# Mask products in pairs, new orders of the attention slots, and block ends without GpSimd's drain, in a one-core attention and routed-expert kernel on Trainium2

## The reference, cut to what matters

```python
def layer(x):                                  # (16, 512, 128)
    n = layernorm(x)
    q, k, v = split(einsum('bsd,ndh->bnsh', n, W_qkv))      # 16 heads of 8
    s = einsum('bnqh,bnkh->bnqk', q, k) / sqrt(8) + causal_mask * -1e10
    x = x + out_projection(softmax(s) @ v, W_out)
    z = layernorm(x)
    p = softmax(z @ Wr + br);  w, i = top_k(p, 2);  w = w / sum(w)
    return x + sum over the 2 chosen experts of w * expert_i(z)
```

## Time and profile before

| what | value |
|---|---|
| runs | 1258.79, 1259.54 and 1265.87 us, median 1259.54 |
| the profiled execution | 1261.42 us, its span 1259.7 us |
| span by stage | attention to about 790 us, tail and routing to 824, experts to 1212, sum to the end |
| PE busy from 50 to 650 us | 582.5 of 600 us, granted clock 1.00 (2.4 GHz) |
| DVE, ACT, POOL busy there | 467.5, 352.5 and 411.8 us |
| one batch (4 slots) in the steady state | 46.1 us for the batch from 484.92 to 531.04 us |

### The profile page before, as it was taken

How to read it: one execution, slowest core, us unless ns; L and a number is a source line. 1 busy time by engine, 2 the same in 40 slices (tenths; PEclk the granted TensorE clock), 3 DMA queues, 4 the chain that set the end, 5 groups by cost and what they waited for, 6 DMA issues and landing times. The chain is left out here.

```text
span 1259.7 us, 27452 instructions
## 1 busy us (share of the span) xinstructions
PE 1118.3 (89%) x8654; PEld 824.5 (65%) x8654; DVE 981.5 (78%) x2792; ACT 759.3 (60%) x1672; POOL 788.7 (63%) x1455
## 2 busy tenths in 40 slices
PE   3899999999999999999999998169999999999920
PEld 2565655655656566566556554169999999999910
DVE  4776877878778778778778873758888888888858
ACT  1465655555556556555555654268888888888800
POOL 2257485686686587677577677616666666666630
PEclk9999999999999999999999998579999999999965
DMA  5223545424424434433433421521111111111138
GB/s 146 92 74 111 175 129 162 133 87 126 137 87 134 124 95 123 130 100 116 135 99 107 130 57 42 153 66 52 52 52 53 52 52 52 52 52 52 31 120 301
DMA packets 138269, 127.37 MB, mean 101 GB/s; under 512 B 71848, under 2 KB 96432, under 8 KB 138128
## 3 DMA queue, kind: packets, MB, share of 16 engines
q1 hardware_dynamic: 127184, 103.59, 27.9%
q0 software_dynamic: 8640, 17.84, 4.4%
q10 hardware_dynamic: 2304, 4.20, 0.9%
HBM read 71.13 MB, written 54.43 MB: 100 GB/s over the span
## 5 line engine op out<-in xcount | busy, mean ns | idle before, releaser
L803 ACT ACTIVATE probs<-st 128x384 f32<-128x384 f32 (+1 forms) x768 | 396.7, 527 | 266.5 <-PE st L704 249.7
L844 DVE TENSOR_REDUCE neg_max<-sa 128x2 fp32r<-128x1024 f32 (+3 forms) x384 | 396.0, 1034 | 99.5 <-PE sa L689 97.5
L645 POOL TENSOR_SCALAR_AFFINE_SELECT probs<-probs 128x128 f32<-128x128 f32 (+1 forms) x768 | 244.2, 333 | 208.3 <-ACT probs L803 202.6
L704 PE MATMUL st<-q_stack,k_pad 128*128 128x256 f32 (+2 forms) x1024 | 355.4, 388 | 8.8 <-DMA q_stack<-max_scratch 6.7
L686 PE MATMUL sa<-k_pad,q_stack 128*128 128x256 f32 (+2 forms) x1024 | 334.7, 369 | 15.0 <-DVE neg_max L844 7.5
L686 PEld LDWEIGHTS sa<-k_pad,q_stack 128*128 128x128 f32 x1024 | 179.7, 191 | 118.1 <-issue 87.2
L704 PEld LDWEIGHTS st<-q_stack,k_pad 128*128 128x128 f32 x1024 | 182.2, 198 | 16.1 <-DMA q_stack<-max_scratch 7.9
L689 PE MATMUL sa<-maskneg,identb 128*128 128x128 bf16 (+1 forms) x768 | 191.6, 249 | 0.0
L1001 POOL DMA_INDIRECT y_scratch<-z,to_row x142 | 168.8, 1189 | 35.9 <-issue 35.9
L1035 PE MATMUL up<-xt_hi,w_cur 128*128 128x256 f32 x568 | 167.3, 295 | 0.0
L717 PE MATMUL pv<-probs,v_aug 128*32 128x512 f32 (+3 forms) x2048 | 167.3, 446 | 0.0
(11 more groups left out here) (159 smaller groups left out, 1536.7 us busy)
## 6 DMA issues: line engine op xcount, KB each, us to landing
q_stack<-q_scratch SPq DMA_DIRECT2D x64, 256.0 KB, 2.7
k_pad<-k_scratch SPq DMA_DIRECT2D x256, 64.0 KB, 2.4
xg<-rows_scratch SPq DMA_DIRECT2D x71, 130.0 KB, 2.1
q_scratch<-q_hi SPq DMA_DIRECT2D x16, 512.0 KB, 3.1
k_scratch<-k_hi SPq DMA_DIRECT2D x16, 512.0 KB, 3.0
y<-y_scratch SPq DMA_DIRECT2D x16, 512.0 KB, 5.4
q_scratch<-q_lo SPq DMA_DIRECT2D x17, 256.0 KB, 3.1
k_scratch<-k_lo SPq DMA_DIRECT2D x17, 256.0 KB, 3.3
```

What stands on the lines that cost most here:

```text
L645: pool.affine_select(out=blk, in_=blk, compare_op=ALU.is_ge, fill=0.0, base=0, pattern=[[0, w], [1, P]], channel_multiplier=-1).then_inc(m ...
L704: last = nc.tensor.matmul(st[:, t % 2, at:at + w], k_pad[:, G * g + j, kk * P:(kk + 1) * P], q_stack[:, g, S - w:S], start=True, stop=True)
L803: nc.scalar.activation(probs[:, n % 2, j, lo:lo + w], st[:, k % 2, at:at + w], ACT.Exp).then_inc(exp_done, 1)
L844: V.tensor_reduce(neg_max[:, n % 2, heads[0]:heads[-1] + 1, i], scores[:, :, 0:(i + 1) * P], AX.X, ALU.max, negate=True).then_inc(sa_read, 1)
```

## The change

Three edits. In `a_step` the first bank's mask product no longer follows the first bank's scores: both mask products come behind the second bank's scores, one after the other. In all four rows of `SLOT` tokens move. And the first two blocks are opened with `no_gpsimd_drain=True`: POOL's DRAIN is gone from their ends, and the four other engines' drains stand there as before.

```diff
-            1: "SR A0 B0 a0 B1 PV0 out S0 A1 B2 a1 B3 mT mE A2 S1 B4 mW a2 B5 A3 S2 B6 a3 B7 ln2 A4 B8 S3 PV1 PV2 PV3 OT a4 B9 mR rs2 A5 B10 RC a5 B11 ON zn",
+            1: "SR A0 B0 a0 Rf B1 PV0 A1 B2 out a1 B3 mT mE A2 S0 B4 mW a2 B5 A3 S1 B6 a3 B7 ln2 A4 B8 S2 PV1 PV2 PV3 a4 OT B9 mR rs2 A5 B10 RC a5 B11 ON zn",
...
-        block = route.enter_context(nc.Block())
+        block = route.enter_context(nc.Block(no_gpsimd_drain=True))
...
-                diagonal = sa[:, s % 2, bank, :].rearrange("p (e k) -> p e k", e=each)[:, :, i * P:(i + 1) * P]
-                last = nc.tensor.matmul(diagonal, identb[:, :], maskneg[:, :].unsqueeze(1).broadcast_to([P, each, P]),
-                                        start=False, stop=True, skip_group_check=True)
                 if bank == 1:
+                    for b2 in range(2):
+                        diagonal = sa[:, s % 2, b2, :].rearrange("p (e k) -> p e k", e=each)[:, :, i * P:(i + 1) * P]
+                        last = nc.tensor.matmul(diagonal, identb[:, :],
+                                                maskneg[:, :].unsqueeze(1).broadcast_to([P, each, P]),
+                                                start=False, stop=True, skip_group_check=True)
                     last.then_inc(sa_written, 1)
...
-        block = experts.enter_context(nc.Block())
+        block = experts.enter_context(nc.Block(no_gpsimd_drain=True))
```

## The result

The changed kernel takes 1244.69 us (median of 4 runs, 1243.33 to 1245.08) beside 1259.95 for the kernel before. The ratio is 0.9851, 95% interval 0.9831 to 0.9871. It is faster by 1.5%, inside the stated range, but the gain is smaller than the forecast 1235: the profiled execution went from 1261.42 to 1244.57, 16.9 us where the sum said 24.7.

The account below looks back on a forecast made before the run. PE was taken to set attention's pace, so gains had to be its idle or hidden lost time; 1.38 us a batch times 15.5 is 21.4, with 3.35 for drains 24.7 off 1261.4, as median 1235 us; range 1211 to 1252.

Parts of the forecast that it names:

- xT: Slot 3's transpose no longer waits for POOL's xn, worked one stage earlier; 0.55 us gained a batch.
- pairs: Attention steps: paired masks leave one exposed weight load instead of two; 0.24 us a slot, 0.54 a batch.
- POOL chain: Slot 1 into slot 2: POOL's work from out to zn sets zT at +15.62; PE's stretch 0.26 us longer.
- drains: Block ends without POOL's drain: 2.9 us gained after the expert block, 0.45 after the first.
- CM: Slot 0: CM behind a4 starts without its gap behind B7; 0.2 us gained a batch.
- PE products at the turn of a slot: Turns of slots 0, 2 and 3: next A0 no longer waits for OT; 0.6 us gained a batch.
- Rival 2: Attention steps: mask pairs save nothing, 8.4 us less gain, about 1243 us; chance 0.15.
- rival 1: Slot 1 to zT: POOL chain does not decide, another 1.24 us a batch gained, about 1216 us; chance 0.16.
- SP's chain: Into B0 of slot 1: later stores, earlier mR and earlier PE add 0.25 us of wait a batch.
- The forecast is wrong if zT does not wait (then it is too slow): PE timeline sign: zT should be the largest wait, near 1 us a batch; otherwise the forecast is too slow.
- Rival 3: Slot 1: AR and XL loads land too late and hold out; about 1276 us if 3.5 us later; chance 0.07.

Follow-up runs that it names:

- e4: Changed kernel with OT back ahead of a4 in all four slots; 1250.82 us, ratio 0.9915 to the kernel before.
- e5: Changed kernel with POOL's scattered stores S0 and S1 directly behind out in slot 1, S4 directly behind S3 in slot 2; 1245.12 us, ratio 0.9828.
- e3: Kernel before with the four new SLOT rows alone, masks and drains as before; 1254.54 us, ratio 0.9937.
- e8: Changed kernel with V behind PV0 in slot 0 and K ahead of a4 in slot 3; 1251.74 us, ratio 0.9902.
- e1: Kernel before with only the two POOL drains left out of the block ends; 1260.23 us, ratio 0.9978.
- e2: Kernel before with only the mask products in pairs, its own slots and drains kept; 1259.94 us, ratio 0.9971.
- b3: Kernel of e7 with store S2 moved from slot 1 to slot 2, S2 to S4 together there; 1239.63 us, ratio 0.9775.
- e7: Changed kernel with SR moved behind mW in slot 0; 1236.52 us, ratio 0.9778 to the kernel before.
- b1: Kernel of e7 with Rf behind mE in slot 1, S2 moved to slot 2, S2 to S4 together there; 1244.28 us, ratio 0.9824.
- b4: Changed kernel with SR behind mW in slot 0 and S4 directly behind S3 in slot 2; 1235.17 us, ratio 0.9766.
- e6: Changed kernel with a4 ahead of PV3 in slots 1 and 2, OT still behind both; 1245.73 us, ratio 0.9843.

## Why the prediction was right, and where its sum was wrong

- **Faster by over 1%:** right, and the range held the time. Of the mechanisms, xT, the pairs, the POOL chain and the drains came about; the turn of slot 2 and CM did not. The sum was 8 us too large. Against before's trace a batch gained 0.53 less than forecast: the turns of slots 0, 2 and 3 fell short by 0.43, CM by about 0.35, and K's copy cost 0.12, while the stretch to zT came out 0.41 better than its two terms.
- **PE products at the turn of a slot, 0.6 a batch:** the step that failed is "With a4 ahead of OT ... A0 of the next slot no longer waits for OT's time". A0 waits for step 4's maximum, 1.23 us of its own; OT in front only added to that. Measured against before, in the mean: slot 0 -0.18, slot 3 -0.12, slot 2 +0.13, so 0.17. In slots 0 and 3 it was CM and K behind a4 that covered the maximum, for with OT in front they still do (e4). In slot 2 A0 still stands 0.67 behind B11, 0.33 more than in slot 3, since a store of POOL ends just before the maximum (e5).
- **CM, 0.2:** its gap went (what follows B7 comes after 0.26 in place of 0.46), but from B7 to A5 slot 0 takes 3.66 us in place of 3.50, and 3.61 with the slots alone (e3). The gap had covered ACT's copy of V: B8 follows A4 after 0.52 in place of 0.36, and with V moved away it is 0.34 (e8). The step put no name to what that gap hid.
- **xT, 0.55:** it came in before's trace, where B5 to xT went from 0.81 to 0.28 in the mean. But in e1, with the same attention, it is 0.28 already, and the turn of slot 2 takes 1.14. The prediction added the two as if each had its own time. Together the turns and xT gained 0.70 against before's trace and 0.77 against e1's, where the forecast had 1.15.
- **Pairs, 0.24 a slot:** right in the sum, wrong in the parts. The first step of slot 1, in the changed kernel:

```profile
522.54 0.42 PE L687 MATMUL sa<-k_pad,q_stack 128*128 128x512 f32 x1
522.80 0.39 PE L707 MATMUL st<-q_stack,k_pad 128*128 128x512 f32 x1
523.02 0.40 PE L687 MATMUL sa<-k_pad,q_stack 128*128 128x512 f32 x1
523.26 0.28 PE L692 MATMUL sa<-maskneg,identb 128*128 128x128 bf16 x2
523.36 0.47 PE L707 MATMUL st<-q_stack,k_pad 128*128 128x512 f32 x1
523.76 0.64 PE L720 MATMUL pv<-probs,v_aug 128*32 128x512 f32 x4
```

  From A0 to PV0 it takes 1.22 us, before 1.36 (519.50 to 520.86). Two masks take 0.10, which is their 256 columns at 2.4 GHz alone, and a full product behind a full one 0.22 to 0.26 in place of 0.31. Over all batches without a wait step 0 gained 0.15 in slots 0 and 1 and 0.07 in slots 2 and 3 (0.08 with pairs alone, e2), steps 1 and 3 gained about 0.07 each, steps 2 and 5 nothing, and step 4 nothing or a loss of up to 0.08. Rival 2 is out: the steps got shorter, and loads for the full array are hidden here behind products of 512 columns, which alone are 0.21. The rule of the Trainium skill ("TensorE: Matmul & The Clock Gate", Part 3, "Packing small matmuls — row/col tiling") that a load overlaps only where row groups differ does not describe these rows.
- **The POOL chain, +0.26:** `out` starts at +3.92 and zT at +15.25 in batches where B0 does not wait (forecast 4.05 and 15.62); from `out` to the end of zn it is 11.2 us, worked out as 11.32. zT follows zn's end by 0.14 to 0.17 in 11 of 12 batches, so the chain does set it, and rival 1 fell. But its wait is short (B5 to zT 0.52 in place of 0.28 in the mean), because PE was held up on its way: A3 of slot 1 by Rf, which stands ahead of step 1's maximum now and had no term, and A0 of slot 2. In b3, where zT does not wait, it comes at +15.1, not at +14.4. The sign "The forecast is wrong if zT does not wait (then it is too slow)" failed: zT's wait came out small and the time was above 1235, not below. A3 in a batch where B0 did not wait (0.19 in the mean of all):

```profile
527.73 0.45 PE L687 MATMUL sa<-k_pad,q_stack 128*128 128x384 f32 x1 [0.46 <-DVE neg_max L847]
```

- **SP's chain, +0.25:** right in sign, by one trace each: B0's wait went from 3.9/11 = 0.35 to 4.9/11 = 0.45 booked. The step named the queue but not the cheap way out, SR behind mW (e7).
- **K behind a4:** no term. K's copy on ACT delays B9's exponential, and B11 waits for it: from A5 to B11 slot 3 takes 1.00 us in place of 0.87, 0.12 of its missing 0.3.
- **Drains, 3.35:** 2.8 by e1's ratio, with 2.9 and 0.2 in its trace and 2.3 and 0.4 in the changed kernel's.
- **Rival 3:** did not come about, and it waited for the wrong load. In the kernel's code XL of a batch loads the x that `out` adds one batch later; only AR's loads belong to the `out` that follows them. The trace agrees: in one batch `out` starts at +5.14 and the XL issued ahead of it lands at +5.34. AR's loads land at +4.25 at the latest, and `out` starts directly behind the zeroing ahead of it in 11 of 12 batches. It starts at up to +5.9 where B0 waits, but B0's wait had moved all of the slot by nearly as much (1.89 of the 1.99).

## What to carry to other kernels

When a wait names an instruction, read that instruction's own length before crediting the edit that clears the queue in front of it: here the 1.2 us of the maximum stayed. Two waits on one path may stand in for one another, so read them in a second trace of the same program before adding them. A gap that goes has to be followed to the next product on each other engine, since short waits hide one another, and an engine that is busy for only 59% of the time, as ACT is here, can be the next one. And in a queue worked in order, a wait for something slow (SR for its stores) belongs behind what is ready (mW).

## What the runs showed of the hardware that was not expected

- A DVE instruction that waited for PE and came due when a scattered store of POOL was ending or had just ended started only about 0.3 us or more behind the store's end: step 4's maximum 0.1 to 0.4 late in slot 2 of the changed kernel, OT 0.2 to 0.8 late in slot 2 of e1. In slot 2 of before, where the store ended 0.4 behind OT's start in most batches, OT was on time. The maximum was on time in all 12 batches when the store was moved (e5, b1, b3, b4). How the one holds up the other is open.
- A DVE subtraction of 128x32 went from 340 to 1169 ns beside four zeroings of POOL in a row (b3) and to 789 and 747 beside two or three (e5, b4), and ended 0.05 to 0.11 us behind the last of them. That the two share something is argued from the times; no run isolates it.
- Splitting PV's run of narrow products by four full ones and their masks cost 0.33 us in each slot so split (e6).
